# The context's key and value projections computed inside the combining stage, its second norm in closed form

## The reference

```
x  = x + tanh(g_ffn[0]) * experts(...)          # two gathered rows of each token
xn = layernorm(x)                               # applied by the outer network
h  = layernorm(xn) * ln_w + ln_b                # layer 1 normalises it again
for kind in q, qx, k, v:                        # fp8 rounding, one scale vector each
    xq = fp8(bf16(clip(h / in_scale[kind], -448, 448)))
    y[kind] = (xq * in_scale[kind]) @ w[kind] * w_scale[kind]
q, qx, k = layernorm over heads of 128, * w + b
kx, vx = context @ w_kv_x                       # 1024 columns each, fp32
kx = layernorm over heads of 128, * w + b
```

## Time and profile before

| | us |
|---|---|
| median of 3 runs | 3654.53 |
| profiled execution | 3659.59 |
| its span | 3657.8 |
| combining stage, 1183.9 to 1390.8 | 206.9 |
| v segment of the projection stage | 70.6 |
| kx segment | 103.5 |
| vx segment | 89.5 |

### The profile page before, as it was taken

How to read it: one execution, slowest core, us unless ns; L and a number is a source line. 1 busy time by engine, 2 the same in 40 slices (tenths; PEclk the granted TensorE clock), 3 DMA queues, 4 the chain that set the end, 5 groups by cost and what they waited for, 6 DMA issues and landing times. The chain is left out here.

```text
span 3657.8 us, 59149 instructions
## 1 busy us (share of the span) xinstructions
PE 3039.5 (83%) x15542; PEld 2339.2 (64%) x15542; DVE 2671.6 (73%) x4860; ACT 2099.3 (57%) x4231; POOL 1516.0 (41%) x1737
## 2 busy tenths in 40 slices
PE   6769996898998005999999789999999999899677
PEld 4546664777887004777778667777777777687433
DVE  7679997666665894666524089999999999624487
ACT  3368885315665223666554278888888888422243
POOL 4300003230000864655544076666666666431265
PEclk9989997998999557999999999999999999999898
DMA  5765663138774755555653332222222222375100
GB/s 197 230 148 150 154 151 102 60 124 273 260 269 154 200 137 152 148 153 172 177 182 116 112 95 68 78 85 85 86 64 82 85 85 62 119 251 193 65 20 23
DMA packets 402746, 490.71 MB, mean 134 GB/s; under 512 B 35908, under 2 KB 251348, under 8 KB 402612
## 3 DMA queue, kind: packets, MB, share of 16 engines
q1 hardware_dynamic: 390660, 440.31, 40.4%
q0 software_dynamic: 11952, 48.78, 3.8%
HBM read 312.69 MB, written 176.31 MB: 134 GB/s over the span
## 5 line engine op out<-in xcount | busy, mean ns | idle before, releaser
L2596 POOL TENSOR_SCALAR h_probs<-h_exp,h_rowsum_inv 128x512 f32<-128x512 f32 x512 | 354.6, 693 | 373.3 <-DVE h_rowsum_inv L2543 302.9
L2502 ACT ACTIVATE h_exp<-h_scores,h_neg_max 128x512 f32<-128x512 f32 x512 | 352.8, 689 | 201.0 <-DVE h_neg_max L2536 200.8
L2460 PE MATMUL h_pT<-ident,h_probs 128*128 128x128 f32 x2048 | 321.8, 280 | 51.3 <-POOL h_probs L2596 40.0
L2536 DVE TENSOR_REDUCE h_neg_max<-h_scores 128x1 f32<-128x512 f32 x512 | 341.5, 667 | 26.4 <-PE h_scores L2452 25.6
L2460 PEld LDWEIGHTS h_pT<-ident,h_probs 128*128 128x128 f32 x2048 | 229.4, 140 | 198.9 <-POOL h_probs L2596 148.7
L2583 POOL TENSOR_TENSOR h_lo<-h_raw,h_hi 128x512 fp32r<-128x512 f32 x256 | 329.5, 1288 | 62.9 <-ACT h_hi L2491 62.9
L2549 DVE TENSOR_TENSOR h_probsT_lo<-h_pT,h_probsT_hi 128x512 fp32r<-128x512 f32 x512 | 345.4, 675 | 0.0
L2175 PE MATMUL g_pQ<-g_w_hi,g_x 128*128 (+1 forms) x640 | 272.4, 426 | 85.2 <-POOL g_w_lo L2306 84.0
L2511 ACT CAST h_probsT_hi<-h_pT 128x512 fp32r<-128x512 f32 x512 | 297.5, 581 | 0.6 <-PE h_pT L2460 0.6
L2279 DVE TENSOR_TENSOR g_normed<-g_pQ,g_rstd 128x512 f32<-128x512 f32 x192 | 132.4, 690 | 186.3 <-PE g_pT L2185 186.2
L2175 PE MATMUL g_pQ<-g_w_lo,g_x 128*128 (+1 forms) x640 | 259.8, 406 | 0.0
(11 more groups left out here) (402 smaller groups left out, 8802.2 us busy)
## 6 DMA issues: line engine op xcount, KB each, us to landing
lnT<-g_out SPq DMA_DIRECT2D x192, 256.0 KB, 2.3
e_w_raw<-in_w SPq DMA_DIRECT2D x24, 1792.0 KB, 7.7
h_raw<-lnT SPq DMA_DIRECT2D x64, 512.0 KB, 5.2
...
b_q_stack<-qk SPq DMA_DIRECT2D x64, 256.0 KB, 7.2
b_k_stack<-qk SPq DMA_DIRECT2D x64, 256.0 KB, 9.0
...
```

The lines of the kernel that those rows point to most:

```text
L2460: last = nc.tensor.transpose(pT[r % 4][:, k], Pn[:, r % 4, bass.ts(k, P)], g["ident"][:])
L2502: nc.scalar.activation(Pr[:, r % 4], pS[r % 2][:], ACT.Exp, bias=nmax[:, r % 4:r % 4 + 1], accum_out=rsum[:, r % 4:r % 4 + 1]).then_inc(ex ...
L2536: v.tensor_reduce(nmax[:, r % 4:r % 4 + 1], pS[r % 2][:], axis=AX, op=ALU.max, negate=True).then_inc(nmax_done.sem, 1)
L2596: nc.gpsimd.tensor_scalar(Pn[:, r % 4], Pr[:, r % 4], rinv[:, r % 4:r % 4 + 1], 1.0, ALU.mult, ALU.mult).then_inc(norm_done.sem, 1)
```

## The change

The combining stage is written anew, without loops, in rounds r = 0 to 16. In round r TensorE makes both vx products of context tile r, transposes the x chunks due, transposes the normalised kx results of r-1, and makes both kx products of r. The 16 weight pieces (vx first, unscaled; kx centred) are split at the stage's start into resident buffers. Two x tiles are combined in each of rounds 0 to 7. Each chunk's clip works in place, the exponent mask works on pairs of bf16 as int32, and the last subtraction moves from GpSimd to VectorE. The second norm goes: with rs1 = (var + eps)^-1/2, rs2 = (rs1^2 var + eps)^-1/2 the row factor is rs1 rs2 and the bias -mean rs1 rs2; GpSimd computes them for two tiles at once, ScalarE applies them. The projection stage loses its kx and vx groups and the context's buffers, loads, casts and subtractions. All else is unchanged.

```diff
+    GROUPS = (14, 15, 12, 13)
...
+    CHUNKS_AT = (0, 0, 0, 1, 1, 1, 1, 1, 1, 2, 1, 2, 1, 2, 1, 1)
...
+    PAIRS_OF_TILES = NT // 2
...
+            def load_w(q):
+                cg, k = GROUPS[q // KT], q % KT
+                if q >= 4:
+                    if q - 4 < 2 * KT:
+                        sp.wait_ge(wv_lo, q - 3)
+                    else:
+                        sp.wait_ge(w_centred, q - 3 - 2 * KT)
+                sp.dma_start(Wr[:, q % 4], wT[:, k, cg * CG:(cg + 1) * CG]).then_inc(w_in[q % 4], 16)
...
+            for q in range(4):
+                load_w(q)
+            load_ctx(0)
...
+            for n in range(2):
+                load_x1(n)
+            for q in range(4, 4 * KT):
+                load_w(q)
+            for r in range(NT + 2):
+                if r + 1 < PAIRS_OF_TILES:
+                    load_x1(2 * r + 2)
+                    load_x1(2 * r + 3)
+                if r + 1 < NT:
+                    load_ctx(r + 1)
+                if 0 <= r - 1 < NT:
+                    store_v(r - 1, 0)
+                    store_v(r - 1, 1)
+                if 0 <= r - 1 < PAIRS_OF_TILES:
+                    store_x2(2 * r - 2)
+                    store_x2(2 * r - 1)
+                if 0 <= r - 2 < NT:
+                    store_k(r - 2, 0)
+                    store_k(r - 2, 1)
+                for c in chunks_at(r - 2):
+                    store_xq(c)
...
+            def gather(n):
+                if n >= 4:
+                    pool.wait_ge(x2_done, n - 3)
...
+                pool.wait_ge(mv_done, 2 * r + 2)
+                steps = (
+                    lambda: nc.gpsimd.tensor_scalar(row[:, 0, c], var, EPS, 0.0, ALU.add, ALU.add),
+                    lambda: nc.gpsimd.tensor_tensor(row[:, 1, c], row[:, 0, c], half, ALU.pow),
+                    lambda: nc.gpsimd.tensor_tensor(row[:, 2, c], row[:, 1, c], row[:, 1, c], ALU.mult),
+                    lambda: nc.gpsimd.tensor_tensor(row[:, 3, c], row[:, 2, c], var, ALU.mult),
+                    lambda: nc.gpsimd.tensor_scalar(row[:, 4, c], row[:, 3, c], EPS, 0.0, ALU.add, ALU.add),
+                    lambda: nc.gpsimd.tensor_tensor(row[:, 5, c], row[:, 4, c], half, ALU.pow),
+                    lambda: nc.gpsimd.tensor_tensor(srow[:, c], row[:, 5, c], row[:, 1, c], ALU.mult),
+                    lambda: nc.gpsimd.tensor_tensor(row[:, 6, c], mean, srow[:, c], ALU.mult),
+                )
...
+            pool.wait_ge(i_in, 16)
+            gather(0)
+            gather(1)
+            ctx_lo(0)
+            for q in range(2 * KT, 4 * KT):
+                w_lo(q)
+            for r in range(NT + 1):
+                if 0 <= r - 1 < NT:
+                    kx_rstd(r - 1, 0)
+                    kx_rstd(r - 1, 1)
+                if r + 1 < NT:
+                    ctx_lo(r + 1)
+                if r + 1 < PAIRS_OF_TILES:
+                    gather(2 * r + 2)
+                    gather(2 * r + 3)
+                if r < PAIRS_OF_TILES:
+                    row_factors(r)
...
+            for r in range(NT + 2):
+                if 0 <= r - 1 < NT:
+                    squares(r - 1, 0)
+                    squares(r - 1, 1)
+                if r + 1 < NT:
+                    ctx_hi(r + 1)
+                if r < NT:
+                    v_copy(r, 0)
+                if 0 <= r - 1 < PAIRS_OF_TILES:
+                    norm(2 * r - 2)
+                    norm(2 * r - 1)
+                if r < NT:
+                    v_copy(r, 1)
+                if 0 <= r - 1 < NT:
+                    affine(r - 1, 0)
+                    affine(r - 1, 1)
+                for c in chunks_at(r):
+                    scale(c)
...
+            def centre(q):
+                j = q - 2 * KT
...
+                v.tensor_reduce(wsum[:, q % 2], raw, axis=AX, op=ALU.add).then_inc(w_link, 1)
+                dve.wait_ge(w_link, j + 1)
+                if j >= 2:
+                    dve.wait_ge(wk_lo, j - 1)
+                v.scalar_tensor_tensor(out=W2[:, q % 2].rearrange("p (h c) -> p h c", h=HC),
+                                       in0=wsum[:, q % 2].unsqueeze(2).to_broadcast([P, HC, DH1]),
+                                       scalar=-1.0 / DH1, in1=raw, op0=ALU.mult, op1=ALU.add).then_inc(w_centred, 1)
...
+            def tile(n):
+                dve.wait_ge(y_in[n % 4], 32 * (n // 4 + 1))
+                v.tensor_tensor(s1[:], Yr[:, n % 4, 0], Yr[:, n % 4, 1], ALU.add).then_inc(t_link, 1)
+                dve.wait_ge(t_link, 2 * n + 1)
+                dve.wait_ge(x_in[n % 4], 16 * (n // 4 + 1))
+                if n >= 4:
+                    dve.wait_ge(xn_done, n - 3)
+                    dve.wait_ge(x2_stored[n % 4], 16 * (n // 4))
+                v.scalar_tensor_tensor(out=X2[:, n % 4], in0=s1[:], scalar=g["tanh_gates"][:, 2:3], in1=X[:, n % 4],
+                                       op0=ALU.mult, op1=ALU.add).then_inc(x2_done, 1)
+                dve.wait_ge(x2_done, n + 1)
+                v.bn_stats(st[:], X2[:, n % 4]).then_inc(t_link, 1)
+                dve.wait_ge(t_link, 2 * n + 2)
+                v.bn_aggr(MV[:, n], st[:]).then_inc(mv_done, 1)
...
+            def to_fp8(c):
+                y, magic = Yb[:, c % 2], Mg[:]
+                dve.wait_ge(y_done, c + 1)
+                v.tensor_scalar(y, y, FP8_MAX, -FP8_MAX, ALU.min, ALU.max).then_inc(q_link, 1)
+                dve.wait_ge(q_link, 4 * c + 1)
+                v.tensor_scalar(magic.bitcast(I32), y.bitcast(I32), EXP2, None, ALU.bitwise_and).then_inc(q_link, 1)
+                dve.wait_ge(q_link, 4 * c + 2)
+                fp8_step(v, 1, y, magic, None).then_inc(q_link, 1)
+                dve.wait_ge(q_link, 4 * c + 3)
+                fp8_step(v, 2, y, magic, None).then_inc(q_link, 1)
+                dve.wait_ge(q_link, 4 * c + 4)
+                if c >= 2:
+                    dve.wait_ge(xq_stored[c % 2], 16 * (c // 2))
+                fp8_step(v, 3, y, magic, Out[:, c % 2]).then_inc(out_done, 1)
...
+            for q in range(2 * KT):
+                wv_low(q)
...
+            for q in range(2 * KT, 4 * KT):
+                centre(q)
...
+            for r in range(NT + 1):
+                if 0 <= r - 1 < NT:
+                    sums(r - 1, 0)
+                    sums(r - 1, 1)
+                if r < PAIRS_OF_TILES:
+                    tile(2 * r)
+                if 0 <= r - 1 < NT:
+                    normalise(r - 1, 0)
+                    normalise(r - 1, 1)
+                if r < PAIRS_OF_TILES:
+                    tile(2 * r + 1)
+                for c in chunks_at(r - 1):
+                    to_fp8(c)
...
+            def kx_transpose(r, h):
+                i = 2 * r + h
+                pe.wait_ge(nr_done, i + 1)
...
+            for r in range(NT + 1):
+                if r < NT:
+                    vx(r, 0)
+                    vx(r, 1)
+                for c in chunks_at(r):
+                    x_transpose(c)
+                if 0 <= r - 1 < NT:
+                    kx_transpose(r - 1, 0)
+                    kx_transpose(r - 1, 1)
+                if r < NT:
+                    kx(r, 0)
+                    kx(r, 1)
...
-    KINDS = (("q", 4), ("qx", 4), ("k", 2), ("v", 2), ("kx", 2), ("vx", 2))
+    KINDS = (("q", 4), ("qx", 4), ("k", 2), ("v", 2))
...
-    NORM = (0, 1, 2, 4)
+    NORM = (0, 1, 2)
...
-            segments(pool, COUNTS, NT, [(rstds, 1), (weights, 0), (context, 1)])
+            segments(pool, COUNTS, NT, [(rstds, 1), (weights, 0)])
```

More of the change, by code:

```diff
@@ L1783, in combine_norm @@
 def combine_norm(nc, g, t):
-    with Mem(nc, "f") as m:
[L1790 to L1955, removed]
-            dve.wait_ge(stored[r], 16 + i * 32 + r4 // 2 * 16)
-            v.scalar_tensor_tensor(out=X2[:, r], in0=s1[:], scalar=g["tanh_gates"][:, 2:3], in1=X[:, r],
-                                   op0=ALU.mult, op1=ALU.add).then_inc(x2_done.sem, 1)
-            dve.wait_ge(x2_done.sem, x2_done.done(n))
-            link(v.bn_stats(st[:, 0], X2[:, r]))
-            m.wait_apart(dve)
-            v.bn_aggr(mv[:, 0, r], st[:, 0]).then_inc(mv1.sem, 1)
-            link.end()
-        def norm(i, r):
-            n = i * 2 + r
-            dve.wait_ge(r1.sem, r1.done(n))
-            v.tensor_scalar(Hn[:, r], X2[:, r], mv[:, 0, r, 0:1], rstd[:, 0, r:r + 1],
-                            ALU.subtract, ALU.mult).then_inc(h_done.sem, 1)
-            dve.wait_ge(h_done.sem, h_done.done(n))
-            v.bn_stats(st[:, 1], Hn[:, r]).then_inc(st2.sem, 1)
-            dve.wait_ge(st2.sem, st2.done(n))
-            m.wait_apart(dve)
-            v.bn_aggr(mv[:, 1, r], st[:, 1]).then_inc(mv2.sem, 1)
-        def norm_again(i, r):
-            n = i * 2 + r
-            dve.wait_ge(r2.sem, r2.done(n))
-            v.tensor_scalar(XN[:, bass.ds(n, 1)].rearrange("p a d -> p (a d)"), Hn[:, r], mv[:, 1, r, 0:1],
-                            rstd[:, 1, r:r + 1], ALU.subtract, ALU.mult).then_inc(n_done.sem, 1)
-        def to_fp8(i, r):
```

(24 more changed lines are left out.)

296 lines of the change are left out of this document (264 added, 32 removed).

## The result

| | us, median | runs |
|---|---|---|
| before | 3654.49 | 4, 3653.81 to 3659.19 |
| after | 3554.01 | 4, 3549.4 to 3555.16 |

What follows compares the result with a forecast made beforehand. It took VectorE to bound the combining stage and TensorE the projection stage's end. Combining +55 (262 against 206.9 us) and projection -196 gave -141 us: 3514 us as a median, range 3486 to 3548.

Steps and rivals of the forecast that it cites:

- Nothing holds that stage but its own loads: Attention stage: only its own loads could delay it, so up to 5 us of loss, inside the range.
- rival D: Longer value-segment drain or later attention start eats the gain, up to 5 us; chance 0.02 with the gain gone.
- the fall to half clock that was priced in: Combining stage, round 1: TensorE idles some 5 us and drops to half clock; round 1 put at 19 us.
- three near limits: Combining stage, rounds 2 to 7: VectorE 13.6, GpSimd 14.1, DMA 14.5 us, so 14.3 us each, 86 us.
- rival B: Combining stage: engine exclusion and DMA add up instead of overlapping; early rounds 17 us, +30, 3544 us; chance 0.26.
- neither enters the sum: Combining stage: VectorE held by GpSimd's long instruction, and the two engines' SBUF contention, both counted as nothing.
- Rival A: Combining stage: TensorE sets every round; rounds 1 to 7 take 87 instead of 105 us, 3489 us; chance 0.20.
- at TensorE's pace: Combining stage, rounds 8 to 15: no gathers or tiles, so TensorE's 12.06 us a round plus transposes, 102 us.
- the sign that the prediction gave for its being wrong: Combining stage: TensorE waiting each late round for a scaling would show the chunks are too dear; no size given.
- -193: Projection stage: the context's two segments, 103.5 + 89.5 us on TensorE alone, are removed.
- Rival C: Combining stage: key transposes wait for VectorE's whole round, 25.7 us a round; +37, 3692 us; chance 0.02.

Runs made afterwards that it cites:

- e1: Changed kernel with 30 VectorE semaphore increments added ahead of its attention loop, nothing else: 3537.67 us, ratio 0.9678 to the kernel before.
- e2: Kernel before with 173 VectorE semaphore increments added ahead of its attention loop: 3687.04 us, ratio 1.0085 to the kernel before.
- e4: Changed kernel with five of nine steps of GpSimd's row factors left out, so part of the computation is missing: 3547.83 us, ratio 0.9703.
- e6: Changed kernel with 30 VectorE increments ahead of the attention loop and the row factor in one power, nothing left out: 3513.81 us, ratio 0.9612.
- e7: The kernel of e6 plus the early clip and mask of e3: 3508.85 us, ratio 0.9598.
- e3: Changed kernel with clip and mask of the first chunk in late rounds moved between VectorE's sums and scaling: 3557.85 us, ratio 0.9726.

## Why the prediction was wrong

**The failed step.** "Nothing holds that stage but its own loads" was said of the attention stage, and only a later start was weighed as rival D, at up to 5 us. Its length was taken as unchanged because its code is. But a change in the number of VectorE's instructions ahead of it moves its loop in the instruction stream, and VectorE is its bound with no idle time. The cost is 25.7 us in the trace, 24.3 of it in 14 stops; e1 takes 25.0 back, and e2 makes 24.5 us of stops in a kernel without the change. No row ahead of the prediction showed the price, but the stage's place as a loop behind edited code was in view. Without it the time would be near 3529 us by the trace (3554.01 - 25.0); e1 measured 3537.67. Both lie inside the range.

**The stage, 277.5 instead of 262.** Counted between the starts of the transposes of successive rounds' keys (some 6 us ahead of the end of a round as the prediction counts), the forecast reads 50 to the first, 86 for rounds 2 to 7, 102 for rounds 8 to 15, 24 at the end. Measured: 50.3, 88.1, 112.3, 26.8.

*Start.* Right in sum, partly by luck. The timeline of TensorE shows the late weights:

```profile
1194.15 0.80 PE L2184 MATMUL f_pV<-f_w_hi,f_ctx_hi 128*128 128x512 f32 x1 [14.18 <-POOL f_ctx_lo L1953]
...
1201.42 0.47 PE L2184 MATMUL f_pV<-f_w_hi,f_ctx_hi 128*128 128x512 f32 x1 [1.93 <-DVE f_w_lo L2094]
...
1212.17 0.79 PE L2184 MATMUL f_pK<-f_w_hi,f_ctx_hi 128*128 128x512 f32 x1 [6.29 <-POOL f_w_lo L1957]
...
1220.72 0.79 PE L2184 MATMUL f_pK<-f_w_hi,f_ctx_hi 128*128 128x512 f32 x1 [3.64 <-POOL f_w_lo L1957]
...
1233.94 0.66 PE L2210 MATMUL f_pT<-ident,f_normed 128*128 128x128 f32 x4 [2.08 <-DVE f_normed L2121]
```

After each of the first, third and fourth gaps a product runs at 0.79 to 0.80 us, the cold rate of the earlier trace rows. The first key product began 28.6 us in (forecast some 25) and round 0 ended some 4 us late, near 42. Round 1 made it up: TensorE idled 2.1 and 0.6 us there, where the prediction had 5, and its key products ran at 0.39 us right behind (from 1235.94), so the fall to half clock that was priced in did not come.

*Rounds 2 to 7.* The size was right (88.1 for 86), the reason only in part, and the agreement is in part luck. The prediction gave three near limits and took one pace of 14.3 us for all six, although two of its limits (VectorE's 13.6 and the DMA's 14.5) hold a chunk that the first of them don't have. Rounds 2 to 4, without a chunk, took 13.1 to 13.6 us and the next three 16.0; these errors cancel. The limit is GpSimd, by e4, at an estimate of 14.1. The two stretches show a round without and one with a chunk:

```profile
1260.70:1273.90 13.20, 12.60 (x63) 10.19 (x61) 7.77 (x12) 8.80 (x14) 11.18 (x19) 1.00 0.77 260
1273.90:1289.90 16.00, 12.63 (x60) 10.21 (x60) 12.97 (x17) 8.67 (x14) 13.99 (x19) 1.00 0.81 258
```

GpSimd's same 19 instructions are 2.8 us longer beside VectorE's chunk, and the round is 2.8 us longer. Groups of after by shape, in the combining stage:

```profile
L1947 POOL DMA_INDIRECT f_routed<-y,f_row_of x32 | 37.0, 1157 | 11.3 <-issue 8.5 <-DMA f_row_of<-row_of 2.9
L1780 DVE TENSOR_TENSOR f_out<-f_y,f_magic 128x2048 f32<-128x2048 bf16 x16 | 36.7, 2292 | 0.5
...
L2121 DVE TENSOR_TENSOR f_normed<-f_pK,f_kx_rstd 128x512 f32<-128x512 f32 x32 | 22.1, 691 | 26.8 <-POOL f_kx_rstd L1967 26.8
...
L2127 DVE TENSOR_TENSOR f_s<-f_routed 128x512 f32<-128x512 f32 x16 | 14.3, 894 | 4.0 <-DMA f_routed<-y,f_row_of 3.9
...
L1976 POOL TENSOR_SCALAR f_row_scale<-f_meanvar 128x2 f32<-128x2 f32 x8 | 6.3, 783 | 2.6 <-DVE f_meanvar L2138 2.4
```

The subtraction on VectorE is 2292 ns for the 2.34 us taken, and the mask 0.69 (L2145) for 0.73. The rule of the Trainium skill that the prediction weighed (VectorE: DVE Perf Modes, "What auto-detection actually checks"), no double rate of a two-input instruction where a tensor is not 16 bits wide, agrees with the 2292 ns; the add of that size, all bf16, takes 1226. VectorE's scaling waits 26.8 us in sum for GpSimd's power. Part of rival B is there, the other way round: VectorE's long instruction holds GpSimd's small one. Timeline of after:

```profile
1267.65 0.26 POOL L1976 TENSOR_SCALAR f_row_scale<-f_meanvar 128x2 f32<-128x2 f32 x1
...
1297.24 2.29 DVE L1780 TENSOR_TENSOR f_out<-f_y,f_magic 128x2048 f32<-128x2048 bf16 x1
1298.06 1.56 POOL L1976 TENSOR_SCALAR f_row_scale<-f_meanvar 128x2 f32<-128x2 f32 x1
```

L1976 ends with the subtraction, after 1.56 us; in the round without a chunk it took 0.26. That hold is 1.3 of the 2.8 us. The four gathers give 1.1 more (5.3 us busy for 4.2), and whether VectorE or their own DMA work lengthens them no run shows. So the term "neither enters the sum" of the prediction's part on engines beside each other was set at nothing and is worth up to 2.8 us a round. Rival A's pace, 12.06 us a round, is nearly reached by e4, e6 and e7, at 12.2 us in three of these rounds.

*Rounds 8 to 15.* The term "at TensorE's pace", 102 us, was under-sized by 10. TensorE's work was sized right (103.0 us busy), but the sign that the prediction gave for its being wrong, TensorE waiting for a scaling in the late rounds, is there, and it makes up in effect all of TensorE's idle time (9.3 us):

```profile
PE f_pT L2210 <- DVE f_normed L2121: 9.7, 11, 2.8
```

The rounds are not free of VectorE: the three with two chunks take 14.3, 15.7 and 15.7 us, and the others 12.2 to 14.1, where the prediction averaged VectorE's 8.5 and 14.2 to 10.7 and let TensorE's pace cover it. Nothing averages them, since the next round's sums and scalings stand behind a round's chunks in VectorE's order. e3 brings the dear rounds to 14.1, the 14.2 that the prediction had for VectorE in such a round, and takes some 4 of the 10 us.

*End.* 26.8 for 24; the step from the last subtraction's end (1452.00) to the next stage's first DMA took 9.1 us for 8.4. The other 2 us are open.

**The projection stage, -201 instead of -196.** The value segment fell from 70.6 to 66.9 us (-3.7 for -3), -193 is as forecast, and the part ahead of the segment, which has the same code, fell by 4.0. That is the scatter between executions: e2, with before's code, has 694.7 us for this stage where before has 699.3, and e1 and e6 have 500.5 and 500.4 where after has 498.2. Against e2's 694.7 the stage is 196.5 us shorter.

**In sum.** The forecast's -141, and then 15.7 for the stage, -5.1 for the projection stage, 25.7 for the attention stage and -0.3 ahead of them: -105.0, the span's difference. That is 36 of the 40 us; the other 4 to 5 come from the 5.1 us that the forecast took off for the median, where after's profiled execution stood only 0.5 above its own. Rival C's circle did not close; it needed 23.2 us a round, and the dearest took 16.0.
